# Two attention layers on one Trainium2 core: layer 0's value products and second-pass steps in another order, and layer 1's second shift transpose one quarter of an item sooner

## The reference

```python
# layer 0
h = concatenate([ctx, x], axis=1)                    # 512 rows a batch
q = x @ q_w + q_b;  k, v = split(h @ kv_w + kv_b)    # 16 heads of 32
attn = softmax(where(mask, q k^T / 32, -inf))
o = (attn v) @ out_w + out_b + x
x1 = gelu(rmsnorm(o) @ mlp_w1 + mlp_b1) @ mlp_w2 + mlp_b2 + x
# layer 1
a = layernorm(ctx) * gamma + beta
attn = softmax(where(mask, (x1 Wq^T)(a Wk^T)^T * 32**-0.5, -inf))
out = x1 + tanh(gate) * ((attn (a Wv^T)) @ Wo^T)
```

## Time and profile before

| | before |
|---|---|
| median of 2 runs | 2437.13 us |
| the profiled execution's own time | 2439.91 us |
| its span, first to last instruction | 2438.1 us |
| mean granted TensorE clock | 0.988 of 2.4 GHz |
| PE busy | 2326.6 us (95%) |
| ACT, DVE, POOL busy | 1434.1, 1059.3, 420.1 us |

### The profile page before, as it was taken

The page is one execution under the profiler, slowest core; times in us unless marked ns, Lnnn a source line. Parts: engine busy times, 40 slices in busy tenths (PEclk is TensorE's granted clock), DMA queues, the critical chain, the costliest instruction groups (busy, mean ns, idle before and its releaser), DMA issues.

```text
span 2438.1 us, 42636 instructions
## 1 busy us (share of the span) xinstructions
PE 2326.6 (95%) x14322; PEld 1863.8 (76%) x14322; DVE 1059.3 (43%) x1942; ACT 1434.1 (59%) x3378; POOL 420.1 (17%) x521
## 2 busy tenths in 40 slices
PE   7999999999999999989999999999999999999998
PEld 6776777777666677768888888888878888888886
DVE  6444445555444444453221221221246556565563
ACT  4766777666666776664222222222237787787876
POOL 4111222222222211130000000000221211212110
PEclk9999999999999999989999999999999999999998
DMA  6444333344434444333110110110244555555553
GB/s 187 106 114 101 95 97 96 99 113 113 113 96 113 96 113 113 86 102 139 52 52 0 52 52 0 52 52 0 87 123 123 133 140 150 130 146 141 135 131 83
DMA packets 141970, 239.11 MB, mean 98 GB/s; under 512 B 25393, under 2 KB 59601, under 8 KB 139873
## 3 DMA queue, kind: packets, MB, share of 16 engines
q1 hardware_dynamic: 140512, 238.05, 37.2%
q10 hardware_dynamic: 1408, 0.41, 0.1%
HBM read 86.28 MB, written 25.21 MB: 46 GB/s over the span
## 4 chain that ended last, share of the span: by engine, by line
PE 40%; SPq 10%; DMA 2%; issue 1%; ACT 1%; DVE 0%; DVEq 0%
SPq L531 9%; PE item_ps L66 5%; PE item_ps L68 5%; PE item_ps L67 5%; PE score_ps L67 5%; PE score_ps L66 5%; PE score_ps L68 5%; PE o_ps L66 3%; PE o_ps L68 3%; PE o_ps L67 3%; PE score_ps L1407 2%; DMA l_stack<-l_qk 1%; PE score_ps L1433 1%; SPq L599 1%; SPq L552 0%
## 5 line engine op out<-in xcount | busy, mean ns | idle before, releaser
L845 ACT ACTIVATE score_ps<-score_ps,l_neg_max 128x512 f32<-128x512 f32 (+1 forms) x1024 | 566.2, 556 | 210.7 <-DVE l_neg_max L1087 202.1
L1087 DVE TENSOR_REDUCE l_neg_max<-score_ps 128x1 f32<-128x512 f32 (+1 forms) x768 | 500.8, 685 | 151.7 <-PE score_ps L1407 149.1
L1868 ACT ACTIVATE mlp_hidden<-score_ps,b_col 128x512 f32<-128x512 f32 x128 | 88.2, 689 | 498.8 <-PE score_ps L68 453.8
L66 PE MATMUL item_ps<-feats_h,weights_l 128*128 128x256 f32 (+1 forms) x1024 | 329.6, 322 | 47.4 <-POOL feats_l L699 21.9
L1407 PE MATMUL score_ps<-l_stack 97*128 97x512 f32 (+1 forms) x1024 | 308.7, 360 | 23.4 <-DMA l_stack<-l_qk 9.4
L68 PE MATMUL item_ps<-feats_h,weights_h 128*128 128x256 f32 (+1 forms) x1024 | 318.6, 311 | 0.0
L67 PE MATMUL item_ps<-feats_l,weights_h 128*128 128x256 f32 (+1 forms) x1024 | 318.5, 311 | 0.0
L1916 DVE TENSOR_TENSOR mlp_hidden_l<-mlp_hidden,mlp_hidden_h 128x512 fp32r<-128x512 f32 x128 | 91.6, 715 | 514.8 <-ACT mlp_hidden_h L1870 514.7
L865 ACT ACTIVATE l_probs<-score_ps 128x1024 f32<-128x1024 f32 x272 | 264.9, 1021 | 59.8 <-PE score_ps L1433 59.5
L66 PEld LDWEIGHTS item_ps<-feats_h,weights_l 128*128 128x128 f32 x1024 | 194.6, 190 | 85.1 <-issue 33.0
L1433 PE MATMUL score_ps<-l_stack 99*128 99x256 f32 x1536 | 243.0, 293 | 10.5 <-ACT l_probs L865 4.6
(11 more groups left out here) (164 smaller groups left out, 4011.4 us busy)
## 6 DMA issues: line engine op xcount, KB each, us to landing
l_stack<-room SPq DMA_DIRECT2D x254, 192.0 KB, 3.1
l_stack<-l_qk SPq DMA_DIRECT2D x254, 128.0 KB
l_stack<-room SPq DMA_DIRECT2D x130, 128.0 KB, 2.9
l_tokens<-in_features SPq DMA_DIRECT2D x16, 1024.0 KB, 4.8
l_stack<-l_qk SPq DMA_DIRECT2D x254, 64.0 KB
l_stack<-room SPq DMA_DIRECT2D x130, 64.0 KB, 2.9
l_rows<-in_x SPq DMA_DIRECT2D x16, 512.0 KB, 4.1
norm_transposed<-norm_room SPq DMA_DIRECT2D x16, 512.0 KB, 4.8
```

The costliest lines, as they stand in the source:

```text
L66: pe.matmul(out, left_l, right_h, start=start, stop=False)
L845: m = act.activation(e, e, ACT.Exp, bias=neg_max[:, q, h:h + 1], accum_out=row_sum[:, q, h:h + 1])
L1087: dve.tensor_reduce(out, bank, AXIS_X, ALU.max, negate=True).then_inc(max_done, 1)
L1868: act.activation(hidden[:, m % HBUF, :], hidden_ps[:, m % 4, :], ACT.Gelu_apprx_tanh, bias=b1_col[:, m:m + 1])
```

## The change

**Layer 0.** `v_ahead` makes only block 0 of tile 2. A new slot "share" comes first: tile 3 of block 0 and tiles 2 and 3 of block 1, then three steps. Two slots "v" make tile 0 and tile 1 whole, with a step ahead of each of the blocks 0, 1 and 2; `v_shared` rises for blocks 0 and 1 inside tile 1. Two slots "late" make tiles 2 and 3 of block 2 and of block 3, each followed by two steps. The five items have three steps each (before, the second had four). DVE copies tile 0 in slot 2, tile 1 in slot 3 and tiles 2 and 3 with item 0. POOL does all four splits ahead of the norm of prev. `turn_norm` and `copy_norm` move from item 1 to item 3, and the wait of `turn_shift` for `nT_done` stays only at half 1; `turn_norm` waits for the shift of half 0 to be copied. In the second pass `shifted` 4 stands ahead of `run(0)`, and every later one is one place further ahead of its run; ACT's exponentials follow. In the last batch the value pieces go tile by tile over 15 steps instead of 12, and DVE's four copies stand at step 19 instead of 16.

**Layer 1.** `turn_shift(1)` stands behind `shifted` 1, a quarter of item 7 sooner, and ACT's copy of it ahead of `exps` 1.

```diff
-    SLOT = ([("values", f) for f in range(FB)] if first else [("share", 0)]) + [("item", k) for k in range(MIXED)]
+    SLOT = [("share", 0)] + ([("v", 0), ("v", 1), ("late", 2), ("late", 3)] if first else [])
+    SLOT += [("item", k) for k in range(MIXED)]
-    STEPS_AT_FIRST = [3, 3, 3, 3, 3, 3, 3, 3, 2] if first else [2, 2, 2, 2, 2, 2, 2, 2]
-    STEPS_IN_SLOT = [3, 3, 3, 3, 3, 4, 3, 3, 3] if first else [1, 1, 1, 1, 0, 3, 3, 2]
+    STEPS_AT_FIRST = [2, 3, 3, 2, 2, 3, 3, 3, 3, 2] if first else [2, 2, 2, 2, 2, 2, 2, 2]
+    STEPS_IN_SLOT = [3, 3, 3, 2, 2, 3, 3, 3, 3, 3] if first else [1, 1, 1, 1, 0, 3, 3, 2]
-    V_AHEAD = FB if first else 2
+    V_AHEAD = 1 if first else 2
+    V_COPIES_IN_SLOT = {2: (0,), 3: (1,), AFTER_T: (2, 3)} if first else {}
-    NORM_SLOT = AFTER_T + 1
+    NORM_SLOT = AFTER_T + 3
...
             def second_pass_of_two_keys(p, a):
                 exps(a, 0)
+                copy_shift(a, 1)
                 exps(a, 1)
-                copy_shift(a, 1)
...
                 exps(a, 3)
-                for g in range(FB - 1):
+                exps(a, KB)
+                for g in range(FB):
                     o_high(a, g)
-                    for s in range(KB * (g + 1), KB * (g + 2)):
+                    for s in range(KB * (g + 1) + 1, min(KB * (g + 2) + 1, PSTEPS)):
                         exps(a, s)
...
-            def values(b, f, step):
-
-                for t in V_ORDER[1:]:
...
+            def v_item(b, t, step):
+
+                at_least(pe, rows_done, QT * (b - 1) + t + 1)
+                pe.wait_ge(low_done, ITEMS * (b + 1) - 1 + t)
+                for f in range(FB):
                     step()
                     n = v_passes(b, t, f)
-                    if f == FB - 1:
-                        n.then_inc(v_done, 1)
-                if f < FB - 1:
-                    n.then_inc(v_shared, 1)
+                    if t == 1 and f < 2:
+                        n.then_inc(v_shared, 1)
+                n.then_inc(v_done, 1)
...
-                if first and norm_banks(a - 1) is o_ps:
+                if first and half == 1 and norm_banks(a - 1) is o_ps:
                     at_least(pe, nT_done, a)
...
                     values_copied(a + 2)
+                    pe.wait_ge(shift_copied, HALVES * (a + 1) + 1)
...
             def groups_of_four_keys(p, a, run, shifted):
+                shifted(a, KB)
                 run(0)
                 for g in range(1, FB):
-                    shifted(a, KB * g)
                     shifted(a, KB * g + 1)
+                    shifted(a, KB * g + 2)
                     if g == 1:
                         items_free(p)
                     project(a, g - 1)
-                    shifted(a, KB * g + 2)
                     shifted(a, KB * g + 3)
+                    if g < FB - 1:
+                        shifted(a, KB * g + 4)
                     run(g)
...
-                    if q == 3 and not first:
+                    if q == 2 and not first:
                         turn_shift(a, 1)
```

More of the change, by code:

```diff
@@ L887, in copy_v @@
             def copy_v(b, t):
-                act.wait_ge(v_done, KB * b + V_ORDER.index(t) + 1)
+                act.wait_ge(v_done, KB * b + t + 1)
                 at_least(act, pv_done, PSTEPS * b)
@@ L1165, in iteration @@
                         low(p, n)
-                    if first and a is not None and slot == VALUE_SLOT:
-                        for t in range(KB):
+                    if a is not None:
+                        for t in V_COPIES_IN_SLOT.get(slot, ()):
                             copy_v(a, t)
@@ L1380, in v_share @@
                 for t in range(PLAIN_V, KB):
-                    if f < V_AHEAD and t == PLAIN_V and not at_first:
+                    if f < V_AHEAD and t == PLAIN_V and (first or not at_first):
                         continue
@@ L1385, in v_share @@
                         n.then_inc(v_done, 1)
-                if f < FB - 1:
+                if f < FB - 1 and (not first or f == 2):
                     n.then_inc(v_shared, 1)
@@ L1506, in groups_of_four_keys @@
                     project(a, g - 1)
-                    shifted(a, KB * g + 2)
                     shifted(a, KB * g + 3)
+                    if g < FB - 1:
+                        shifted(a, KB * g + 4)
                     run(g)
             def last_batch_of_four_keys(a, stack, run, shifted):
-                pieces = iter([(t, f) for f in range(FB) for t in V_ORDER[1:]])
+                pieces = iter([(t, f) for t in range(KB) for f in range(V_AHEAD if t == PLAIN_V else 0, FB)])
                 def next_of_v():
@@ L1517, in next_of_v @@
                         pe.wait_ge(o_low_done, FB * a)
-                    elif f == 0:
+                    elif f == 0 and t < PLAIN_V:
                         pe.wait_ge(rows_done, QT * (a - 1) + t + 1)
@@ L1524, in last_batch_of_four_keys @@
                 for k in range(AHEAD, STEPS):
-                    if k < AHEAD + 3 * FB:
+                    if k < AHEAD + KB * FB - V_AHEAD:
                         next_of_v()
@@ L1573, in iteration @@
                         turn_norm(prev)
-                    if kind == "values":
-                        values(a, n, step)
+                    if kind == "v":
+                        v_item(a, n, step)
+                    elif kind == "late":
+                        v_share(a, n)
                     elif kind == "item":
```

16 lines of the change are left out of this document (4 added, 12 removed).

## The result

The kernel after takes 2366.35 us (two runs, 2365.28 and 2367.42) against 2437.13 us before: a ratio of 0.971, 95% interval 0.9668 to 0.9751. That is 70.8 us less. The forecast was 2379.0 in a range from 2366 to 2403. Four more runs, reported last among the experiments, have a median of 2364.9 us, 1.1 us outside it. That it came inside at all is luck.

A forecast was written before the change was run, and what follows sets the result against it. PE's work plus its waits, with the loss in layer 0's period, bounds the kernel. Gains of 47.6 + 0.3 + 0.5 + 10 = 58.4 us off 2439.9 gave 2381.5, less 2.8 for the median, rounded to 2379; range 2366 to 2403, its own 2368 to 2391.

The forecast's parts named there:

- The stall at `scores` 8: Layer 0's period: a new PE wait at step 8 for the sum of step 4, costing 0.4 us.
- The value copies: Layer 0, item 0: PE's wait for DVE's copy of the value tiles goes, 1.62 us a period.
- The splits: Layer 0, item 0's block 3: PE's 1.22 us wait for POOL's splits goes, with 0.4 us to spare.
- ACT's exponentials: Layer 0, into the second pass: shorter DVE-ACT chain with three-step items and later norm, 0.5 us more gain, bounds 0 and 0.9.
- `shifted` 4 ahead of `run(0)`: Layer 0's second pass: it fills 0.48 of 0.81 us at `weigh` 3; gain 0.3 us, bounds 0 and 0.5.
- From `shifted` 7 to the scores: Layer 0's period end: SP's stack load sets 14.5 us whatever PE does; PE's wait grows from 0.64 to about 1.5 us.
- The sum: Layer 0's gain per period: 3.7 us by the steps, 3.4 taken, bounds 2.2 and 4.1; times 14, 47.6 us.
- First batch: Layer 0's first iteration: PE's wait of up to 5.1 us for POOL has a fixed end; only 0.3 us gained.
- Last batch: Layer 0's last batch: time change taken as -0.5 us, from +3 to -4, depending on where the low clock falls.
- Layer 1: Layer 1: earlier turn removes `shifted` 4's DMA waits and `scores` 8's wait, partly given back; gain 10 us, bounds 5 and 14.
- The stack isn't the bound: Rival, layer 0: SP starts sooner and the three run stalls count too; 4.3 us a period, 2366 us, chance 0.09.
- The norm wasn't in SP's way: Rival, layer 0: stack queued in SP's order behind the later `turn_norm`; 1.0 us a period left, 2415 us, chance 0.04.

## Why the prediction was right, and where it was off

The prediction's A is 566.42 us in the kernel before; all positions here are counted from it or from the A of the kernel named.

*What bounds the kernel* held: the time is PE's work plus its waits in layer 0's period, and 60 of 75 us came from there.

*The stall at `scores` 8* held: due at A + 7.15, it came at 7.13.

*The value copies* held: item 0's block 0 was due at A + 17.1 and came at 17.17. The kernel with the copies late shows their price from the other side, 2.35 us and a clock at risk.

*The splits* held, in time and in place: due to end at A + 19.3, ended at A + 19.37, and the 1.22 us went. For item 5 I had 2.9 to 3.0 us without the chain; without the norm's 0.42 it was 3.1. The difference fits the 0.2 us of unhidden weight loads that I added to the new order: the stumbles went, and none came in their place.

*ACT's exponentials*, the step that failed in its reason. I took 0.5 us for a chain that four-step items make longer and that the norm's early copy held back. A four-step item costs nothing; the norm's place alone is worth 0.75 us up to `shifted` 7. The upper bound of 0.9 covered it, by luck: the reason behind it was the chain and the norm together, and only the norm was there.

*`shifted` 4 ahead of `run(0)`*: taken 0.3, measured 0.38 to 0.41, shown from both sides.

*From `shifted` 7 to the scores* held: the way stayed 14.7 us (14.5 in the prediction, which counts from the end of `shifted` 7's last matmul) and the wait for the stack grew to 1.3 to 1.6 idle. "SP's own pace" was only part of the reason: the issues take 10.7 us, and the rest is transfers that land. "Whatever PE does" is right for the order of PE's work; a wait for fewer transfers shortens it.

*The sum* is the term that was mis-sized. By my steps it was 3.7 us a period, I took 3.4 for meetings within 0.1 to 0.4 us that then cost nothing, and 4.24 was measured: above even the bound of 4.1. So 14 periods gave 60.3 us where I took 47.6; 1.0 of it is extra in the first of them, whose way from `shifted` 7 took 15.65 us before and 14.68 after. The 0.84 us are some 0.2 up to item 5, 0.25 of the norm, 0.1 of the second pass's order, and the 0.3 of caution.

*First batch*: 2.1 us for 0.3. The wait for POOL shrank only from 5.1 to 4.7, but the stretch at the low clock that starts beside it went from 10.2 to 3.4 us. How long it is varies: in the second profile of the same kernel it is 6.8 us, beside a wait of 3.45. So this gain is in part chance. *Last batch*: 1.2 for 0.5.

*Layer 1*: 12.1 for 10, inside the bounds. Thirteen steady batches gave 0.43 each, 5.6 in all, as derived. The give-back came, but not at the turn: in a steady batch PE doesn't wait at `turn_shift` (the waits for `l_shift` are in the last batches), and most of what `scores` 8 gains is gone by `shifted` 0, ahead of the turn, in three places where a matmul follows the one before it 0.1 us later. The first batch gave 4.65 where I had 2.7: some 1.8 for the wait and 1.3 for the low stretch of 3.4 us behind it, as derived, and 1.55 because the stretch at layer 1's start was 3.4 us instead of 6.8, which the edit doesn't touch. The end gave 1.8.

*The rivals.* "The stack isn't the bound" named 2366 and a gain of 4.3 a period, the very numbers that came. Its mechanism didn't: the runs' stalls bring nothing in either kernel, and the way from `shifted` 7 didn't move. A number that agrees is no proof of the reason that came with it. The norm wasn't in SP's way: SP issues the stack's mask 0.46 us behind the start of `shifted` 7's last matmul, as before. The wait of 1.3 to 1.6 us for the stack didn't lower the clock, as forecast, but with 0.1 us to spare: at 1.70, 1.72, 1.83 and 2.24 us the same wait did in other kernels, for 1.6 us a time where I had 5.2. The forecast's "between 1.6 and 2.2" was right.

## What to carry to other kernels

Measure stalls from start to start, and when a long wait goes, count the short losses beside it. When several transfers share one semaphore and the first users need only some, give these a semaphore of their own: it turned a wait that no order of PE's work could shorten into none, for 22 us. A helper engine's late work (here POOL's norm ahead of two splits) costs its wait plus what the clock loses behind it (here 3.7 and 3.0 us a period), so order such an engine's queue by who waits.

## What the runs showed of the hardware

- The clock after a wait inside dense work: up to 1.68 us idle at layer 0's scores, no fall; 1.70 to 2.24 us, a fall to 0.50 for 3.4 us in four of seven; 2.2 us at item 0, the same in one period of two; 3.0 us with 0.4 to 1.1 more close behind, a fall for 6.8 us in each of 14. A stretch of 3.4 us cost 1.4 to 1.6 us.
- One queue's issues: 0.67 us each for 16 in a row with 576 KB per j and 0.65 with 320, most of them 0.64 apart in both. While ScalarE issued four more, 12 took 9.3 us on the mean, with single ones held for up to 1.7 us in the period shown. With fewer bytes the last issue's data landed 2.0 us behind the issue's start, with all of them 3.3. Why single issues of SP are held was not settled; none was with fewer bytes.
